# Attention scores as 32-partition f32 products in four row groups, division after a transpose, and elimination steps spread over more rounds

## What is computed

```
q, k, v = split(modulate(layernorm(x)) @ W_qkv + b_qkv)       # per sequence: 128 x 144 each
scores = einsum('blhd,bmhd->bhlm', q * 9 ** -0.5, k)           # 16 heads, 128 x 128
attn = softmax(scores)                                         # maximum subtracted
x = x + gate_msa * (einsum('bhlm,bmhd->blhd', attn, v) @ W_proj + b_proj)
x = x + gate_mlp * (gelu(modulate(layernorm(x)) @ W_fc1 + b_fc1) @ W_fc2 + b_fc2)
U, _ = qr(P)                                                   # P 144 x 64
R = expm(A(cond))                                              # 64 x 64, skew, per sequence
x = x + ((x @ U) @ R - x @ U) @ U.T
```

## Time and profile before

| | |
|---|---|
| Median of 3 runs | 362.62 us (361.86 to 363.21) |
| The profiled execution | 363.15 us, of which the span is 361.4 us |
| PE busy | 318.2 us (88%), 3935 products (passes) |
| DVE busy | 256.6 us (71%) |
| ACT busy | 187.2 us (52%) |
| POOL busy | 146.2 us (40%) |
| Mean granted clock of PE | 0.948 of full speed |

### The profile page before, as it was taken

The page is one execution under the profiler, slowest core; times in us unless marked ns, Lnnn a source line. Parts: engine busy times, 40 slices in busy tenths (PEclk is TensorE's granted clock), DMA queues, the critical chain, the costliest instruction groups (busy, mean ns, idle before and its releaser), DMA issues.

```text
span 361.4 us, 10608 instructions
## 1 busy us (share of the span) xinstructions
PE 318.2 (88%) x3935; PEld 245.4 (68%) x3935; DVE 256.6 (71%) x1063; ACT 187.2 (52%) x403; POOL 146.2 (40%) x421
## 2 busy tenths in 40 slices
PE   0598989889989899999999999999987957999995
PEld 0472668567877788787778777777776643467784
DVE  7381036688899989887786878988988576664243
ACT  1222464347766557567685676776762233623221
POOL 3512124235355454553543535545543508720000
PEclk9998765769999999999999999999999899999999
DMA  8817000000000000000000000000000000000013
GB/s 198 233 19 261 4 1 2 3 1 2 2 3 2 2 5 3 2 2 3 2 3 2 5 2 2 0 5 0 2 3 3 2 3 0 2 0 2 0 34 100
DMA packets 8765, 8.28 MB, mean 23 GB/s; under 512 B 1042, under 2 KB 8312, under 8 KB 8586
## 3 DMA queue, kind: packets, MB, share of 16 engines
q1 hardware_dynamic: 8006, 6.78, 6.5%
q10 hardware_dynamic: 708, 0.83, 0.8%
HBM read 6.40 MB, written 1.20 MB: 21 GB/s over the span
## 4 chain that ended last, share of the span: by engine, by line
PE 61%; DVE 18%; ACT 8%; issue 5%; POOL 4%; DMA 2%; ACTq 1%; DVEq 0%; POOLq 0%
PE bank L1255 5%; PE bank L1492 5%; PE bank L1284 4%; PE bank L1476 3%; PE bank L1318 3%; PE bank L1171 3%; PE bank L1273 3%; PE bank L1308 3%; PE bank L1300 3%; PE bank L1244 3%; PE bank L1245 2%; PE bank L1179 2%; PE bank L1274 2%; ACT KT L626 2%; PE bank L1263 2%
## 5 line engine op out<-in xcount | busy, mean ns | idle before, releaser
L440 POOL TENSOR_TENSOR root<-rec,mhalf 128x1 f32<-128x1 f32 x64 | 34.6, 540 | 107.5 <-DVE Z L922 107.5
L984 DVE TENSOR_REDUCE nmax<-bank 128x4 f32<-128x512 f32 x64 | 43.0, 672 | 34.5 <-PE bank L1263 34.2
L616 ACT ACTIVATE E<-bank 128x512 f32<-128x512 f32 x64 | 38.0, 594 | 40.6 <-PE bank L1274 40.2
L626 ACT ACTIVATE KT<-bank 64x512 bf16<-64x512 bf16 x64 | 37.5, 587 | 0.8
L1273 PE MATMUL bank<-QT,KT 128*128 128x128 bf16 x256 | 36.7, 224 | 0.0
L1274 PE MATMUL bank<-NMT,headsel 128*128 128x128 bf16 x256 | 36.3, 222 | 0.0
L1308 PE MATMUL bank<-Z,sel 128*128 128x128 f32 x128 | 29.5, 314 | 6.9 <-DVE Z L928 6.8
L1284 PE MATMUL bank<-E,V 128*32 128x128 f32 x512 | 27.9, 291 | 5.4 <-ACT E L616 5.4
L622 ACT ACTIVATE QT<-bank 128x512 bf16<-128x512 bf16 x32 | 19.0, 595 | 26.1 <-PE bank L1255 26.0
L1273 PEld LDWEIGHTS bank<-QT,KT 128*128 128x128 bf16 x256 | 24.3, 99 | 10.0 <-issue 10.0
L1308 PEld LDWEIGHTS bank<-Z,sel 128*128 128x128 f32 x128 | 20.9, 200 | 14.7 <-issue 13.6
(11 more groups left out here) (270 smaller groups left out, 827.5 us busy)
## 6 DMA issues: line engine op xcount, KB each, us to landing
gates<-gates_dram SPq DMA_DIRECT2D x1, 2304.0 KB, 8.4
x_all<-in_x_dram SPq DMA_DIRECT2D x4, 288.0 KB, 7.6
out_dram<-x_all SPq DMA_DIRECT2D x8, 144.0 KB, 2.0
wskew<-in_L_cond_W_dram SPq DMA_DIRECT2D x4, 283.5 KB
wada<-in_L_cond_W_ada_dram ACTq DMA_DIRECT2D x1, 432.0 KB
wfc1a<-in_L_cond_W_fc_dram SPq DMA_DIRECT2D x1, 288.0 KB
wfc2a<-in_L_cond_W_fc_dram SPq DMA_DIRECT2D x1, 288.0 KB
wproj<-in_L_cond_W_proj_dram SPq DMA_DIRECT2D x16, 5.1 KB
```

Source lines behind the costliest of these rows:

```text
L440: link(nc.gpsimd.tensor_tensor(root[:, at], rec[:, at], mhalf[:, 0:1], ALU.pow))
L616: nc.scalar.activation(E[:, q, :, :].rearrange("p i t -> p (i t)"), bank[4][:, :], ACT.Exp).then_inc(s_E, 1)
L626: nc.scalar.activation(KT[parity][n][own, p, :, :].rearrange("p g t -> p (g t)"), bank[2][own, 256:512].bitcast(BF16), ACT.Copy).then_inc( ...
L984: nc.vector.tensor_reduce(nmax[:, q % 2, 4 * (q // 2):4 * (q // 2) + 4], bank[3][:, :].rearrange("p (i m) -> p i m", i=4), AX.X, ALU.max, ...
```

## The change

- **Scores.** The splitting is gone. q and k of four heads lie in a stack of 4 x 32 columns, each head 9 features and zeros (`SL = 32`), and an f32 transpose of 128 columns brings them to four groups of 32 partitions. `scores(b, g)` and `scores_T(b, g)` are eight f32 products for eight heads, four row groups into four banks (0 to 3), so a round has two of each in place of four. DVE takes one maximum over 1024 columns, ACT one exponential over 1024. Both kinds of scores use the same banks 0 to 3.
- **Maximum.** DVE writes the negated maximum as a tenth feature of q (the keys' tenth is one). The stack is transposed a second time (`queries_again_T`), and the transposed scores come out with the maximum subtracted. POOL clears the column.
- **Division.** The values are written as 16 slots of 16 rows for all heads (8 products in each of two blocks, pairs adding into one place), a tenth row holds the sum. Two f32 transposes bring them back to time on partitions (`heads_back`), the reciprocal is 128x16, the multiply 128x144, and two more transposes (`normalized_T`) precede a projection of two products.
- **Elimination steps.** The table STEPS gives four steps to each of the rounds -2, -1 and each even round, three to odd ones. The selecting column is read with stride zero from the identity, so `sel` is gone. Row products share bank 7 with `heads_back` and the projection.
- **Generator.** The stages come one round later (rounds 1 to 11), between `values(b - 1, 0)` and step 2 of a round, in banks 4 and 5; `bank5_read` holds what is transposed into bank 5 until they are read.
- W_proj is loaded by 3 transfers in place of 17.

The diff, cut to its core:

```diff
-    SL = 64
+    SL = 32
...
+    VS, VO = 48, 16
...
+        STEPS = {}
+        for b in range(-2, B + 1):
+            for q in range(4):
+                if len(STEPS) <= RD and (b < 0 or q < 3 or b % 2 == 0):
+                    STEPS[b, q] = len(STEPS)
...
-        POWER, HALVES, ODD, SQUARE = 2, 5, 6, 7
+        POWER, HALVES, ODD, SQUARE = 3, 6, 7, 8
...
+        def scored(n):
+            return banks[:, 0:4, 0:256]
...
-            def rest(b, which, stack):
...
-            def low(b, which, stack):
...
-            def selector(k, n):
...
+            def column_cleared(b):
+                pool.wait_ge(s_qmT, b + 1)
+                nc.gpsimd.memset(qstk[b % 2][:, :, D:D + 1], 0.0).then_inc(s_qz, 1)
...
+            def stacked(b):
...
+                nc.scalar.activation(qstk[b % 2][:, :, 0:D], per_head(0), ACT.Copy, scale=SCALE).then_inc(s_stk, 1)
+                nc.scalar.activation(kstk[:, :, 0:D], per_head(1), ACT.Copy).then_inc(s_stk, 1)
+                wait(act, s_pv, 2 * b - 4)
+                nc.scalar.activation(V[b % 3][:, :, VO:VO + D], per_head(2), ACT.Copy).then_inc(s_V, 1)
+
+            def exponentials(b, g):
+                act.wait_ge(s_ST, 2 * b + g + 1)
+                wait(act, s_pv, 2 * b - 1 + g)
+                nc.scalar.activation(E[:, g, :, :, :].rearrange("p r j t -> p r (j t)"), scored(g), ACT.Exp).then_inc(s_E, 1)
...
+            def maximum(b, g):
+                dve.wait_ge(s_S, 2 * b + g + 1)
+                wait(dve, s_qmT, b - 1)
+                nc.vector.tensor_reduce(qstk[b % 2][:, 8 * g:8 * g + 8, D:D + 1].rearrange("p (j r) a -> p r (j a)", r=4),
+                                        scored(g).rearrange("p r (j m) -> p r j m", j=2),
+                                        AX.X, ALU.max, negate=True).then_inc(s_max, 1)
...
-                nc.vector.reciprocal(rsum[:, :], bank[6][:, 0:128]).then_inc(s_rsum, 1)
...
-                TT(ON[:, :, :].rearrange("p q t -> p (q t)"), Osb[:, :], bank[6][:, :], ALU.mult).then_inc(s_on, 1)
+                slots = bank[7][:, 256:512].rearrange("p (h s) -> p h s", h=H)
+                link(nc.vector.reciprocal(rsum[:, :].rearrange("p (h a) -> p h a", a=1), slots[:, :, D:D + 1]))
+                TT(ON[:, :].rearrange("p (h d) -> p h d", h=H), slots[:, :, 0:D],
+                   rsum[:, :].rearrange("p (h a) -> p h a", a=1).to_broadcast([128, H, D]), ALU.mult).then_inc(s_on, 1)
...
-            def maxima_parts(b):
...
+            def bank5_read(b):
+                wait(pe, s_KT, min(b + 2, B))
+                if b == 1:
+                    pe.wait_ge(s_rsq, 1)
+                if b == 2:
+                    pe.wait_ge(s_Bs, 1)
+                if power(b):
+                    pe.wait_ge(s_N, b - POWER + 1)
+                if b == HALVES:
+                    pe.wait_ge(s_ev, 6)
+                if b == ODD:
+                    pe.wait_ge(s_X, 1)
+                    pe.wait_ge(s_Y, 1)
+                if squaring(b):
+                    pe.wait_ge(s_X, b - SQUARE + 2)
...
+            def scores(b, g):
...
+                for j in range(2):
+                    for r in range(4):
+                        rows = slice(32 * r, 32 * r + 32)
+                        ins = mm(bank[r][:, 128 * j:128 * j + 128], QT[rows, 2 * g + j, :], KT[b % 3][rows, 2 * g + j, :],
+                                 start=True, stop=True)
                 ins.then_inc(s_S, 1)
...
+            def scores_T(b, g):
+
+                pe.wait_ge(s_QM, b + 1)
+                pe.wait_ge(s_max, min(2 * b + 3 + g, 2 * B))
+                wait(pe, s_E, 2 * b + g)
+                for j in range(2):
+                    for r in range(4):
+                        rows = slice(32 * r, 32 * r + 32)
+                        ins = mm(bank[r][:, 128 * j:128 * j + 128], KT[b % 3][rows, 2 * g + j, :], QM[rows, 2 * g + j, :],
+                                 start=True, stop=True)
                 ins.then_inc(s_ST, 1)
...
-            def sums(b):
...
-            def division(b):
...
+            def row_bank(k, b):
+                wait(pe, s_Gstep, min(k, RD))
                 wait(pe, s_Bstep, k - 1)
...
+            def heads_back(b):
+                pe.wait_ge(s_O, b + 1)
+                wait(pe, s_pr, b)
...
+            def projection(b):
+                pe.wait_ge(s_oT, 2 * b + 2)
+                mm(bank[7][:, 256:256 + C], oT1[:, :], wproj1[:, :], start=True, stop=False)
+                mm(bank[7][:, 256:256 + C], oT2[:, :], wproj2[:, :], start=False, stop=True).then_inc(s_proj, 1)
+
+            def step(b, q, before=None):
+                k = STEPS.get((b, q))
+                if k is not None or before:
+                    last = k if k is not None else max([n for at, n in STEPS.items() if at < (b, q)]) + 1
+                    row_bank(last, b)
+                if before:
+                    before(b - 2)
+                if k is None:
+                    return
+                if k < RD:
+                    mm(bank[7][:, 0:2 * RD], ident[:, k:k + 1].to_broadcast([128, 128]), Z[:, 0:2 * RD],
+                       start=True, stop=True).then_inc(s_Grow, 1)
+                if k > 0:
+                    mm(bank[7][:, 2 * RD:3 * RD], ident[:, k - 1:k].to_broadcast([128, 128]), Z[:, 2 * RD:3 * RD],
+                       start=True, stop=True).then_inc(s_Brow, 1)
...
+            def attention(b):
+                if scoring(b):
+                    scores(b, 0)
+                if b >= 3:
+                    pe.wait_ge(s_pr, b - 2)
+                step(b, 0)
+                if closing(b):
+                    values(b - 2, 1)
...
+                if prepares(b):
+                    qkv(b + 1)
...
+                if weighing(b):
+                    scores_T(b - 1, 0)
+                step(b, 1, heads_back if closing(b) else None)
...
+                if prepares(b):
+                    keys_T(b + 1)
+                    queries_T(b + 1)
...
+                if scoring(b):
+                    scores(b, 1)
+                if weighing(b):
+                    values(b - 1, 0)
+                generator_stage(b)
...
+                if closing(b):
+                    pe.wait_ge(s_on, b - 1)
+                step(b, 2)
+                if closing(b):
+                    bank5_read(b)
+                    normalized_T(b - 2)
...
+                if weighing(b):
+                    scores_T(b - 1, 1)
+                step(b, 3, projection if closing(b) else None)
...
+                    queries_again_T(b)
+                if normalizing(b):
...
+                    inputs_T(b + 2)
...
+                if b == -1:
+                    pe.wait_ge(s_v, 4)
+                    windows(0, 32)
+                if b == 0:
+                    windows(32, RD - 1)
```

752 lines of the change are left out of this document (314 added, 438 removed).

## The result

The changed kernel takes **376.82 us** (median of 4 runs, 375.42 to 378.12) against 362.38 us of the kernel before on the same chip: a ratio of 1.040, interval 1.035 to 1.044, so 4.0% slower. 357.5 us was forecast, with a range up to 371, and the time lies outside it. The profiled execution took 378.12 us with a span of 376.3; the forecast stands for a span of about 356.

A forecast was written before the change was run, and what follows sets the result against it. PE, busy 91 to 95% of steady rounds, was taken as the bound, with DVE soon met. Terms -5.4, -5.3, +1.8, -6.4 and +9.9 sum to -5.4 from 363.15: 357.7, stated as 357.5 us, range 344 to 371.

The forecast's parts named there:

- the walks: Chains of waits between PE and DVE followed through each stage; a steady even round 12.15 us, an odd one 10.95.
- I charge 2 us in all: Rounds 2 to 7: PE stands 2 to 3.5 us in five rounds, lowering the granted clock; 2 us charged.
- the clock falls: Slower rival: in rounds 2 to 7 PE's stands bring half-speed stretches, giving 366 to 370 us; chance 0.15.
- The start (+9.9): From 33.2 us through round 1: lone early steps, then `windows` at 5.08 us; 59.5 us for 49.6.
- Rounds 2 to 7 (+1.8): Generator stages and `bank5_read` delay PE: walked 86.1 us for 86.3, plus 2 us for the clock.
- Rounds 8 to 11 (-5.3): 52.6 us for 57.9; squaring's two blocks take 2 us, of which about 1.6 lengthens each round's chain.
- Rounds 12 to 15 (-5.4): Steady rounds of 12.15 and 10.95 us, round 15 about 10 without QKV: 45.2 us for 50.6.
- DVE's two maxima and PE's projection: Both on a round's chain, said to keep the mean round at 11.55 us, above PE's 9.5 of work.
- The end (-6.4): 277.6 to 299.0 us: smaller reciprocal, no division on PE, halved projection, fewer score blocks; 15 us for 21.4.
- The weight loads: Slower rival: in all four score blocks f32 loads don't overlap, a block takes 1.1 us, total 371; chance 0.13.
- signs named as right: Score blocks 0.5 to 0.65 us, rounds 12 and 13 23 us, projection released by Z, round 0 57 to 61, PE busy 275.
- signs named as wrong: Blocks over 0.75 us, clock below 0.8 in rounds 2 to 7, round 0 before 54, steady rounds under 10.5 or ACT-set.

The follow-up runs named there:

- e1: Changed kernel plus unread 128-column f32 products wherever PE stands (rounds -2 and -1, later waits, the end): 367.5 us, 1.011 of the kernel before.
- e3: Changed kernel plus unread 128-column products only in rounds 14 to 17 and ahead of the last phase's products: 374.6 us.
- e8: Changed kernel with attention output and projection in bank 6, plus four unread 128-column products ahead of each step of rounds -2 and -1: 353.4 us.
- e13: Changed kernel, banks as they are, plus four unread 128-column products ahead of each step of rounds -2 and -1 only: 370.7 us.
- e5: Changed kernel with only the spread of steps undone, four in every round from 0 to 15: 370.3 us.
- e10: Changed kernel with attention output and projection in bank 6 and four steps in every round from 0, no unread products: 352.4 us.
- e7: Changed kernel with the transposed attention output and the projection's product both moved to bank 6: 360.5 us, 0.988 of the kernel before.

## Why the prediction was wrong

Against the profiled execution (span 376.3 for about 356) 20.3 us were missed. The lower clock cost at least 11.8 us for the 2 that were charged, so some 10 of the 20 are the clock's; the other 10 are errors of the walks, the largest in rounds 2 to 7 and at the end. Neither theory holds alone. These shares come from one profiled execution of each kernel.

**The clock (term: "I charge 2 us in all").** This is the step that failed most: 2 us in rounds 2 to 7 and, beyond what the start already had, nothing elsewhere. By stage, the changed kernel against the runs that were granted the clock there, it cost 4.7 us up to round 0 and 3.8 in rounds 2 to 7 (e1), 1.5 from round 15 to the products and 1.8 in the last phase (e3). That is 11.8 us, with the added products' own work left in, so the clock's price is rather higher. As a whole, e1 gave back 9.3 us, since its products cost time where the clock was full already.

The rival "the clock falls" had 0.15 and named the mechanism rightly (a stand of PE in rounds 2 to 7, then a fall). It was still too narrow, since it looked for falls in rounds 2 to 7 only. Of the 51 us more at the lower level, some 24 are the end's (27.3 for the 3.4 that a clock of 0.92 is in 21.4 us), some 19 those of rounds 2 to 7 (a clock of 0.90 in 94.4 us) and the rest is spread. The argument against it, "the clock stayed at 1.00 from 82.8 to 277.6 in spite of gaps up to 1.4 us", was read right, but the stands of 2 to 4 us that the same text forecast were outside what it covers.

**The start (+9.9).** Direction right, 14.0 measured (63.6 for 49.6). `windows` was priced at 5.08 us and took 6.9; e8's 4.29 shows that this term has the clock inside it. Of the 4.1 us missed, the 3.2 up to round 0 are the clock's: with the early products round 0 starts at 57.50 (e13) and 58.95 us (e1), sooner than the 60.5 of the forecast. That the spread steps cost more at the start than they save later was in the working (+9.9 against 1.2 us a step) but was hidden by the sum; e5 and e10 measure it as a loss of 6.5 and 8.1 us.

**Rounds 2 to 7 (+1.8).** Measured +8.1. The waits behind `bank5_read` were foreseen at 3 to 4 us and came at 4.1, 3.2 and 3.2. With the clock at 1.00 (e1) the stage is 90.6 us, wide products included, so the clock cost at least 3.8 us, 1.8 more than was charged. The walk itself gave 86.1, up to 4.5 us too little. In e1 rounds 3 and 7 take 14.2 and 16.1 us for 11.6 and 13.7 in the walk, and the other four together what was walked; which of their waits was missing I didn't take apart.

**Rounds 8 to 11 (-5.3).** Measured -2.9 at full clock, so no question of the clock. The mis-sized term is the squaring's two blocks, of which 1.6 us a round were put on the chain. PE's timeline shows them at 2.0 us start to start, with 0.29 of wait ahead of them for ACT's copy of the queries. From step 0 to step 0 these rounds take 14.18, 13.10, 14.43 and 13.10 us, on average 1.98 us more than the 12.26 and 11.19 of steady rounds without squaring. So all of the 2 us stood on the chain, 1.5 us too little in four rounds; most of the rest is the steady round itself, 0.1 to 0.2 us longer than walked.

```profile
213.00 1.15 PE L1086 MATMUL banks<-Xm,Ym 64*64 64x64 f32 x32 [0.29 <-ACT QT L493]
213.95 1.13 PE L1086 MATMUL banks<-Ym,Xm 64*64 64x64 f32 x32
215.01 0.49 PE L1324 MATMUL banks<-Z,ident 128*128 128x128 f32 x2
```

**Rounds 12 to 15 (-5.4).** The walk held: 11.19 and 12.26 for 10.95 and 12.15, -3.7 in all. Of the 1.7 missed, 0.65 is round 12's first score block, which stands in the stage as measured but ahead of step 0, where the walk begins; round 15 took 10.5 for "about 10". What the walk took as given is what e7 removed: that the projection waits for Z and step 0 for the projection. I had named "DVE's two maxima and PE's projection" as the chain; of these the projection's place was a choice of a bank.

**The end (-6.4).** Measured -2.3. e3 gives this stretch the full clock and gets back 1.4 of its 19.1 us. The other 2.7 are the walk's own error; which of its waits was too short I didn't take apart.

**The weight loads**, the other slower rival, are out: a block of 0.65 is below the 0.75 from which it would have decided.

**The signs.** Of the signs named as right, the block (0.65), rounds 12 and 13 together (23.5 us) and the projection's wait for Z came; round 0 at 57 to 61 us (63.67) and PE busy near 275 us (309.6) didn't. None of the signs named as wrong appeared: in rounds 2 to 7 the clock was 0.90, and the sign was a clock below 0.8. A clock of 0.90 is 19 of the 94 us at the lower level, and these already cost 3.8 us or more, so the sign was set too far out.

## What to carry to other kernels

Before the work on an engine is counted, list for each buffer that changes place which waits it inherits from its new neighbours: two outputs in the wrong banks cost 16 us here, more than the 14.4 us by which the changed kernel is slower. When a change thins TensorE's work, price every long stretch at both clock levels, and do it stage by stage: where another engine sets the pace the lower level is nearly free (e3), and elsewhere it isn't (e8). Steps moved to where nothing runs beside them cost their full latency, 2.5 to 2.9 us for what costs 1.1 to 1.2 in a full round.
